# Another build of the node table and the edge records, and two loads per item in the edge loop, in a graph attention and mixture-of-experts kernel

## The chip, the cores and the metric

One core of one Trainium2 chip. The metric is the time of one execution of the program on the device, in microseconds (us), the median of several runs without a recording. Lower is better.

## What is computed

A graph attention layer and then a mixture of experts, each added to its input. The part that the change touches is the first:

```python
x = x + gnn(layernorm(x), edge_attr_16, edge_attr_4, W_n, attn_l, attn_r, attn_m, src, dst)   # 6250 x 256, 200000 edges, dst sorted
x = x + ffn(layernorm(x), router_w, w1, w2, w3)                                             # 8 experts, the best 2

def gnn(feat, e_pro, mask, W_n, attn_l, attn_r, attn_m, src, dst):
    feat_src = (feat @ W_n).reshape(N, 8, 32)
    el = einsum('nhd,hdt->nht', feat_src, attn_l)
    er = einsum('nhd,hdt->nht', feat_src, attn_r)
    em = einsum('ef,hft->eht', e_pro, attn_m)                # e_pro: 16 features of an edge
    e = (einsum(el[src], mask) + einsum(er[dst], mask) + einsum(em, mask)) / 3   # mask: 4 of an edge
    e = where(e > 0, e, 0.2 * e)
    e_exp = exp(e - segment_max(e, dst)[dst])
    a = e_exp / segment_sum(e_exp, dst)[dst]
    return segment_sum(feat_src[src] * a[:, :, None], dst)
```

## The kernel before, in words

Everything is float32. The nodes lie in 49 blocks of 128. Semaphores order the engines; there is no planner, each engine's program is written out by hand. What stands on a queue (SP's and ACT's DMA issues among it) runs in the order of the program, and an instruction that waits holds back all behind it.

*Stage 1, the table build (lines 199 to 490).* SP loads dst, then x (`xall`) in one DMA and its last block in another, W_n and router_w, src, and then edge chunks. ACT issues 24 small DMAs of constants (`bd`, `bm`). PE waits for all 26 of `w_in` (line 442) before it makes the projection weights `wall`. DVE finds which edge begins a node (`pen`), makes 5 of 49 counts, takes `bn_stats` of all 49 blocks (line 398), joins them (`join_stats`), and ACT takes one root over all (line 330). Then block by block: DVE normalizes (`norm`, line 405), PE transposes (`turn`, line 462), ACT copies (`copy_xt`, line 334), PE projects (line 468), DVE copies out (`rows_out`, line 410) to `fo`, of which there are two, and SP stores to `table` in DRAM (line 283). A norm is two blocks ahead of its copy-out. Into the loop are woven 44 more counts on DVE, `count` (line 390): how many dst in a row of 1600 are below a block's end. Every second block there is a chunk of 100 edge columns: SP loads 16 features and 4 mask values per edge, ACT packs (`pack`, lines 348 to 352) src, dst, penalty, an empty word, the mask and the features to records of 24 words, SP stores them to `rec_d`. There are 16 chunks; the program order of SP is two table stores, a chunk store, a chunk load.

*Stage 2 (lines 494 to 635).* PE sums the counts, and a short chain on PE and DVE makes the list of items: 256 successive edges each, 832 of them, which may begin anywhere in the records (`start_i`) and belong to one block (`blk_i`). Then eight w2 matrices are transposed on the way from DRAM to DRAM.

*Stage 3, the edge loop (lines 644 to 1203).* It is unrolled: 52 batches of 16 items. `slot(i, w)` is a batch's turn on each engine. SP's slot (line 796): `records` loads the records of batch +3, item by item (`load_records`, lines 770 and 771: it reads the item's start into a register, checks it, computes an address, issues a DMA of 128 x 192 B), after ACT's `unpack` of the batch before; `penalties` loads `pen_in_rows`; `targets` stores what DVE took out of the records and loads it again, broadcast, as `dst_row`. For `dst_row` waits ACT's `compare` (line 943). POOL gathers table rows for 16 items, two indirect DMAs an item (line 819), at most 36 items ahead of PE's sums. ACT's `unpack` (lines 992 to 998) copies the mask and the features of a batch out of the records, and PE's `turn_e16` (line 826) transposes the features. DVE weighs the gathered rows, PE sums them by one-hot matrices (line 862), DVE adds to the accumulator (line 1163).

*Then* come the router, the sorting of nodes to experts, and the expert tiles. None of it is changed.

## Time and profile before

| | us |
|---|---|
| median of 3 runs (lowest, highest) | 4086.85 (4086.71, 4087.13) |
| the profiled execution's own time | 4127.28 |
| its span | 4125.6 |
| table build, about | 0 to 228 |
| items and w2 | 228 to 291 |
| edge loop | 291 to 2930 |
| router, sorting, experts | 2930 to 4125.6 |

| | PE | weight loads | DVE | ACT | POOL |
|---|---|---|---|---|---|
| busy us in the span | 3054.4 | 2356.6 | 1979.3 | 1623.2 | 1857.8 |
| share | 74% | 57% | 48% | 39% | 45% |

The profile is of one execution of the program. Engines are PE (matmul), PEld (its weight load), DVE, ACT, POOL, and SP, which issues DMAs; a q behind a name (SPq) is the engine's sequencer. "L771" is line 771. In a row of the timeline stand the start, the length, the engine, the line, the operation, the tiles written and read, how many of them were merged (x16), and in brackets how long the engine had been idle and what ended it. "remote" and "issue" stand there where the profile shows no cause. Register steps, semaphore waits and DMA issues are not counted as busy time.

### The profile page before, as it was taken

To read this page: it belongs to the slowest core of one execution; us is meant where nothing else is said; L and a number is where in the kernel's file an instruction comes from. 1 tells how busy PE (TensorE), PEld (TensorE's weight loads), DVE (VectorE), ACT (ScalarE), POOL (GpSimd) and SP (SyncE) were. 2 spreads that over 40 slices of the span, in tenths; PEclk is the share of its full clock that TensorE was granted. 3 is DMA by queue.
4 is the path that set the end of the run, shared out by engine and by line. 5 is a ranking of instruction groups with operands and counts; after the bars stand their busy time and mean duration, and the time that the engine had idled before them with its cause. 6 is when DMAs were issued, how large, how long until landed. Compare 5 with 4: busy or idle time off the path is not lost. (4 is left out here: it accounts for less than half of the span.)

```text
span 4125.6 us, 59259 instructions
## 1 busy us (share of the span) xinstructions
PE 3054.4 (74%) x12566; PEld 2356.6 (57%) x12567; DVE 1979.3 (48%) x5348; ACT 1623.2 (39%) x3631; POOL 1857.8 (45%) x1906
## 2 busy tenths in 40 slices
PE   3541777776777777777677776777765999999997
PEld 1221666565556665665566655555553677777775
DVE  6730555555555555555555555555673122222221
ACT  2311544454455444545544544455432222222221
POOL 0005456666666665666665666666254111111111
PEclk9865677777777777777767778777855999999998
DMA  7834444444444444444444444446564312121123
GB/s 221 258 138 112 123 140 130 131 128 129 131 129 130 131 130 128 132 138 130 130 131 129 130 130 130 130 129 119 75 216 136 91 31 32 31 32 31 31 32 83
DMA packets 309415, 481.35 MB, mean 117 GB/s; under 512 B 161911, under 2 KB 237507, under 8 KB 300366
## 3 DMA queue, kind: packets, MB, share of 16 engines
q0 software_dynamic: 100848, 285.40, 28.1%
q1 hardware_dynamic: 194910, 181.82, 14.5%
q10 hardware_dynamic: 13392, 11.23, 0.9%
q8 instruction: 89, 1.46, 0.2%
q14 instruction: 176, 1.44, 0.1%
HBM read 408.52 MB, written 76.12 MB: 117 GB/s over the span
## 5 line engine op out<-in xcount | busy, mean ns | idle before, releaser
L819 POOL DMA_INDIRECT rows<-table,idx x1664 | 1575.6, 947 | 1063.3 <-issue 445.9
L862 PE MATMUL ps_acc<-rows,hot 128*128 128x264 f32 x3328 | 1260.7, 516 | 538.5 <-DVE acc L1163 496.5
L862 PEld LDWEIGHTS ps_acc<-rows,hot 128*128 128x128 f32 x3328 | 761.9, 253 | 673.1 <-issue 566.6
L1163 DVE TENSOR_TENSOR acc<-acc,ps_acc 128x264 f32 x832 | 355.3, 427 | 987.3 <-remote 659.3
L847 PEld LDWEIGHTS ps_term<-er,hot_t 128*128 128x128 f32 x3328 | 638.1, 247 | 218.5 <-issue 146.5
L847 PE MATMUL ps_term<-er,hot_t 128*128 x3328 | 579.5, 305 | 85.7 <-issue 67.9
L1149 DVE TENSOR_TENSOR rows<-rows,ps_p 128x512 f32<-128x512 f32 x832 | 565.5, 680 | 3.8 <-ACT ps_p L971 0.5
L960 ACT ACTIVATE hot<-iota_row,neg_rel 128x128 f32<-128x128 f32 x1664 | 546.3, 388 | 8.7 <-PE ps_acc L862 8.0
L1730 PE MATMUL ps_h<-w,acc 128*128 x1680 | 528.5, 457 | 0.5 <-ACT acc L1649 0.5
L1642 POOL DMA_INDIRECT x_dram<-acc,to x105 | 161.7, 1540 | 761.8 <-ACT acc L1658 761.8
L935 ACT COPY e_t<-ps_e 128x128 f32<-128x128 f32 x208 | 56.4, 271 | 1021.6 <-remote 978.1
L1730 PEld LDWEIGHTS ps_h<-w,acc 128*128 128x128 f32 x1680 | 302.5, 190 | 158.5 <-issue 36.2
L1743 PE MATMUL ps_y<-w2s,acc 128*128 x1260 | 312.1, 390 | 7.5 <-DMA w2s<-w_t 6.6
L1698 DVE COPY acc<-ps_g 128x256 f32<-128x256 f32 x105 | 44.6, 425 | 521.7 <-PE ps_g L1737 521.7
L1743 PEld LDWEIGHTS ps_y<-w2s,acc 128*128 128x128 f32 x1260 | 231.7, 190 | 85.7 <-issue 43.4
L943 ACT ACTIVATE hot_t<-dst_row,neg_part 128x1024 f32<-128x1024 bf16 x208 | 239.1, 1149 | 34.8 <-DMA dst_row<-rel_d 34.7
L1658 ACT ACTIVATE acc<-ps_y,gate 128x256 f32<-128x256 f32 x105 | 49.8, 475 | 476.2 <-PE ps_y L1743 476.2
L965 ACT ACTIVATE hot<-hot 128x1024 f32<-128x1024 f32 x208 | 219.7, 1056 | 5.0
L949 ACT ACTIVATE hot_t<-hot_t 128x1024 f32<-128x1024 f32 x208 | 217.0, 1043 | 0.2
L839 PE MATMUL ps_term<-bm,e_t 128*128 128x256 f32 x416 | 190.6, 554 | 31.6 <-ACT e_t L935 31.6
L1711 DVE TENSOR_TENSOR acc<-acc,ps_h 128x341 f32<-128x341 f32 x210 | 97.6, 506 | 179.0 <-PE ps_h L1730 179.0
L1666 ACT ACTIVATE acc<-ps_h 128x341 f32<-128x341 f32 x210 | 84.1, 453 | 219.5 <-PE ps_h L1730 219.5
(263 smaller groups left out, 2811.9 us busy)
## 6 DMA issues: line engine op xcount, KB each, us to landing
dst_row<-rel_d SPq DMA_DIRECT2D x52, 1024.0 KB
rows<-table,idx POOLq DMA_INDIRECT x1664
rec<-rec_d SPq DMA_DIRECT2D x832, 24.0 KB
rec_d<-acc SPq DMA_DIRECT2D x16, 1050.0 KB
acc<-slots_x SPq DMA_DIRECT2D x105, 130.0 KB, 2.1
acc<-in_edge_attr_dram SPq DMA_DIRECT2D x16, 700.0 KB
wrow<-in_L_ffn_w_dram ACTq DMA_DIRECT2D x16, 640.0 KB
table<-fo SPq DMA_DIRECT2D x49, 148.0 KB
```

Of the source, the lines that this page charges most:

```text
L819: pool.indirect_dma_start(rows[:, in_ring(k) + j, :], None, table, bass.IndirectOffsetOnAxis(ap=idx[w][:, t:t + 1], axis=0)).then_inc(gath ...
L839: pe.matmul(ps_term[s % 2][:, 0:QT * HT], e16_t[s % 2][:, :], bm[:, :, :].rearrange("p t d -> p (t d)"), start=True, stop=False)
L847: last = pe.matmul(ps_term[s % 2][:, t * HT:(t + 1) * HT], hot_t[s % 2][:, t, :], flat(er[:, ds(b, 1), :]), start=False, stop=(t == QT - 1))
L862: last = pe.matmul(ps_acc[m % 2][:, 0:PW], hot[m // QI % 2][:, m % QI * G + j, :], rows[:, in_ring(i * (2 * NI) + at) + j, 0:PW], start=(j ...
L943: act.activation(hot_t[s % 2][:, :, :], dst_row[s // QUADS][:, s % QUADS * QT:(s % QUADS + 1) * QT, :], ACT.Square, bias=neg_part[:, 0:1]) ...
L949: act.activation(hot_t[s % 2][:, :, :], hot_t[s % 2][:, :, :], ACT.Relu, bias=1.0, scale=-1.0).then_inc(item_made, 1)
L960: act.activation(hot[m // QI % 2][:, t % QT, :], iota_row[:, :], ACT.Square, bias=neg_rel[m // NI][:, t:t + 1]).then_inc(square_ok, 1)
L965: act.activation(hot[s % 2][:, :, :], hot[s % 2][:, :, :], ACT.Relu, bias=1.0, scale=-1.0).then_inc(hot_ok, 1)
L1149: dve.tensor_tensor(r, r, p4, ALU.mult).then_inc(msg_ok, 1)
L1163: dve.tensor_tensor(so_far, so_far, ps_acc[m % 2][:, 0:PW].rearrange("p (h d) -> p h d", h=HEADS), ALU.add).then_inc(added, 1)
L1730: last = pe.matmul(ps_h[2 * m + half][:, 0:HALF], xt[v][:, k * P:(k + 1) * P], flat(w13[:, ds(e, 1), at:at + HALF]), start=(k == 0), stop= ...
L1743: last = pe.matmul(ps_y[:, 0:DIM], ht[v][0:w, c * P:(c + 1) * P], flat(w2s[0:w, ds(e, 1), c * DIM:(c + 1) * DIM]), start=(c == 0), stop=(c ...
```

## The change

- x is loaded in seven groups of seven blocks, each on a semaphore of its own, group 0 as the very first DMA, W_n and router_w right behind it. Statistics, joining, root and reciprocal are made per group: `spread(g)` on DVE after the copy-out of block 7(g-1)+1, `root(g)` on ACT, `roots(g)` on DVE three blocks later.
- The edge features are copied from the input to `e16_d` inside DRAM, in eight DMAs that ACT issues (`copy_e16`), five behind the last five packs and three at the start of stage 2. Records have 8 words; a chunk has 200 columns; there are eight, one every five blocks.
- The counts of odd blocks are made on ACT, as a sum of signs (`Sign` with a threshold lowered by one half, and an accumulator), and repaired in stage 2: s/2 + 800. None is made ahead of the loop.
- `fo` has four buffers; the loops of the build are unrolled.
- In the edge loop SP gets `features(i, w)`: 16 further loads (a register read, a check, an address, a DMA of 128 x 128 B) between `records` and `penalties`, for batch +2. The records' DMAs are 128 x 64 B. ACT unpacks the mask alone. PE's `turn_e16` waits for the features' DMAs.

The diff, cut to its core:

```diff
-CHUNK = 100
+CHUNK = 200
-RC = 4 + T + F
+RC = 4 + T
-EARLY = 5
+FO = 4
+CHUNK_EVERY = 5
+ACT_COUNTS = range(1, BLOCKS, 2)
+E16_PARTS = 8
+E16_EARLY = 5
...
+        def copy_e16(eng, n):
+            lo, hi = n * (EDGES // E16_PARTS), (n + 1) * (EDGES // E16_PARTS)
+            eng.dma_start(e16_d[lo:hi, :].rearrange("r f -> (r f)").rearrange("(a n) -> a n", a=200),
+                          edge16[lo:hi, :].rearrange("r f -> (r f)").rearrange("(a n) -> a n", a=200)).then_inc(e16_out, 16)
...
@@ SP, table build
+                    load_x(0)
+                    sp.dma_start(wall[:, :, 0:DIM], w_n.rearrange("(k p) d -> p k d", p=P)).then_inc(w_in, 16)
+                    sp.dma_start(rt_rows[:, :], router_w).then_inc(w_in, 16)
+                    sp.wait_ge(dst_none, 4)
                     sp.dma_start(dst_sb[0:1, 1:COLS + 1], dst[0:COLS].unsqueeze(0)).then_inc(dst_in, 16)
...
+                    load_x(1)
                     for part_of in SPREAD:
                         sp.dma_start(src_sb[part_of, :], src.rearrange("(p t) -> p t", p=EP)[part_of, :]).then_inc(src_in, 16)
+                    for c in range(2):
+                        load_chunk(c)
+                    for g in range(2, GROUPS):
+                        load_x(g)
+                    for b in range(BLOCKS):
                         sp.wait_ge(f_sb, b + 1)
+                        sp.dma_start(table[b * P:(b + 1) * P, :], fo[:, b % FO, :]).then_inc(f_out[b % FO], 16)
+                        c = chunk_after(b - 1)
+                        if c is not None:
+                            store_chunk(c)
+                            if c + 2 < CHUNKS:
+                                load_chunk(c + 2)
...
@@ ACT, table build
+                    for b in range(BLOCKS):
+                        if b + 2 < BLOCKS:
+                            copy_xt(b + 2)
+                        if b % BC == 2 and b // BC + 1 < GROUPS:
+                            root(b // BC + 1)
+                        c = chunk_after(b)
+                        if c is not None:
+                            pack(c)
+                            if c >= CHUNKS - E16_EARLY:
+                                copy_e16(act, c - (CHUNKS - E16_EARLY))
+                        if b in ACT_COUNTS:
+                            act.wait_ge(signs_ok, ACT_COUNTS.index(b))
+                            count(b)
...
@@ DVE, table build
+                    for b in range(BLOCKS):
+                        if b + 2 < BLOCKS:
+                            norm(b + 2)
+                        if b not in ACT_COUNTS:
+                            dve.wait_ge(cnt_ok, counted)
+                            count(b)
+                            counted += 1
+                        rows_out(b)
+                        g = b // BC + 1
+                        if g < GROUPS:
+                            if b % BC == 1:
+                                spread(g)
+                            if b % BC == 4:
+                                roots(g)
...
@@ ACT, stage 2
+                    for n in range(E16_EARLY, E16_PARTS):
+                        copy_e16(act, n)
...
@@ SP, edge loop
+                    def features(i, w):
+                        after_apart(sp, e16_ps, batches(i, w, QUADS, QUADS))
+                        for u in range(NI):
+                            k0 = sp.value_load(start_i[0:1, ds(batches(i, w, NI, 2 * NI + u), 1)], min_val=0, max_val=EDGES)
+                            sp.dma_start(of_item(e16[w], u).rearrange("p j f -> p (j f)"),
+                                         e16_d[ds(k0, ITEM), :].rearrange("(p j) f -> p (j f)", j=G)).then_inc(e16_in[w], 16)
...
                         if is_batch(i, w, 3):
                             records(i, w)
+                        if is_batch(i, w, 2):
+                            features(i, w)
                         if is_batch(i, w, 1):
                             penalties(i, w)
...
                     load_records(0, 0)
+                    sp.wait_ge(e16_out, 16 * E16_PARTS)
                     all_slots(slot)
...
@@ PE, edge loop
-                        pe.wait_ge(taken_ok, (i + r) * 2 + (s // QUADS + 1))
+                        pe.wait_ge(e16_in[s // QUADS], 16 * NI * (i + r + 1))
...
@@ ACT, edge loop
                         after(act, term_used, batches(i, w, QUADS, QUADS))
-                        after(act, e16_ps, batches(i, w, QUADS, QUADS))
-                        act.copy(mask[w][:, :, :], rec[w][:, :, RC - F - T:RC - F])
-                        act.copy(e16[w][:, :, :], rec[w][:, :, RC - F:RC]).then_inc(taken_ok, 1)
+                        act.copy(mask[w][:, :, :], rec[w][:, :, RC - T:RC]).then_inc(taken_ok, 1)
```

## Rows read from the trace of the kernel before

**Rows 1.** Stretches: length, busy us per engine (instructions), granted clock, DMA share, GB/s.

```profile
112.00:160.00 48.00, 22.94 (x70) 12.62 (x71) 32.56 (x71) 19.79 (x42) 0.00 (x0) 0.81 0.97 309
...
200.00:245.00 45.00, 22.31 (x76) 10.26 (x76) 30.93 (x76) 3.38 (x10) 1.66 (x5) 0.84 0.16 52
```

**Rows 2.** Waits of ACT, 54 to 215 us: in total, times, longest.

```profile
ACT acc L348 <- DMA acc<-in_edge_attr_dram: 59.8, 14, 5.8
```

**Rows 3.** Timeline of the start: start, length, engine, line, operation, idle before.

```profile
9.14 4.75 ACTq L316 DMA_DIRECT2D bm<-in_L_gnn_attn_m_dram  x8
...
32.39 1.09 PE L445 MATMUL ps_w<-ident,wall 128*128 128x128 f32 x4 [32.39 <-DMA rt_rows<-in_L_ffn_router_w_dram]
...
36.43 0.19 ACT L328 COPY rt<-ps_f 128x16 f32<-128x16 f32 x1
...
53.82 0.74 DVE L405 TENSOR_SCALAR xn<-xall,mv,rstd 128x256 f32<-128x256 f32 x2
```

**Rows 4.** Groups by line and shape, 0 to 470 us: count | busy, mean ns.

```profile
L390 DVE TENSOR_SCALAR_CACHE_REDUCE junk<-dst_sb,thr 128x1600 f32<-128x1600 int32 x49 | 91.7, 1872 | 0.1
...
L352 ACT COPY acc<-acc 125x1600 f32<-125x1600 f32 x16 | 24.3, 1518 | 0.0
...
L398 DVE BATCH_NORM_STATS2 stats<-xall x49 | 16.1, 409 | 8.8 <-DMA xall<-in_x_dram 8.8
...
L330 ACT ACT_TABLE_LOAD x1 | 1.3, 1283 | 0.0
```

**Rows 5.** Timeline of DVE in the build: first copy out, both paces, last.

```profile
58.47 0.42 DVE L410 COPY fo<-ps_f 128x256 f32<-128x256 f32 x1 [2.98 <-PE ps_f L468]
...
62.39 0.42 DVE L410 COPY fo<-ps_f 128x256 f32<-128x256 f32 x1 [2.98 <-PE ps_f L468]
...
205.24 0.42 DVE L410 COPY fo<-ps_f 128x256 f32<-128x256 f32 x1
...
208.12 0.42 DVE L410 COPY fo<-ps_f 128x256 f32<-128x256 f32 x1
...
227.14 0.42 DVE L410 COPY fo<-ps_f 128x256 f32<-128x256 f32 x1 [0.92 <-DMA table<-fo]
```

**Rows 6.** DMA issues: count, KB each, us from issue to landing.

```profile
out_dram<-x_dram SPq DMA_DIRECT2D x1, 6250.0 KB, 21.8
```

**Rows 7.** Timeline of SP's queue at the loop's start.

```profile
292.43 41.52 SPq L771 DMA_DIRECT2D rec<-rec_d  x32
...
341.02 0.70 SPq L794 DMA_DIRECT2D dst_row<-rel_d  x1
352.25 61.25 SPq L771 DMA_DIRECT2D rec<-rec_d  x16
...
416.44 0.34 SPq L794 DMA_DIRECT2D dst_row<-rel_d  x1
```

**Rows 8.** Timeline of POOL at the loop's start.

```profile
314.05 1.02 POOL L819 DMA_INDIRECT rows<-table,idx  x1 [26.79 <-DVE idx L1065]
...
392.88 0.95 POOL L819 DMA_INDIRECT rows<-table,idx  x1 [0.30 <-issue]
```

**Rows 9.** Line 771, 292 to 314 us: ns min/median/max, first and last start.

```profile
L771 SPq FUSED_REGOPS  x20: 42/42/47, 292.3 to 313.6; - x20
```

**Rows 10.** The same line, 344 to 403 us.

```profile
L771 SPq MOVE rec<-rec_d x7: 690/700/1387, 350.8 to 400.0; - x7
```

**Rows 11.** Timeline of SP's queue in the steady loop.

```profile
1510.47 36.96 SPq L771 DMA_DIRECT2D rec<-rec_d  x16
...
1562.10 35.72 SPq L771 DMA_DIRECT2D rec<-rec_d  x16
```

**Rows 12.** Groups of POOL, 500 to 2700 us.

```profile
L819 POOL DMA_INDIRECT rows<-table,idx x1413 | 1338.0, 947 | 863.7 <-remote 398.4 <-issue 377.0 <-PE ps_acc L862 88.3
```

**Rows 13.** Timeline of all engines at one pause of the loop.

```profile
1548.58 0.43 DVE L1163 TENSOR_TENSOR acc<-acc,ps_acc 128x264 f32 x1 [4.12 <-remote]
...
1549.18 0.95 POOL L819 DMA_INDIRECT rows<-table,idx  x1 [2.76 <-remote]
```

More of the change, by code:

```diff
@@ L226, in gnn_moe_kernel, with chunk_after @@
             f_ps, f_sb = sem("f_ps"), sem("f_sb")
-            f_out = [sem("f_out0"), sem("f_out1")]
+            f_out = [sem(f"f_out{u}") for u in range(FO)]
+            def chunk_after(b):
+                c, left = divmod(b, CHUNK_EVERY)
+                return c if left == 0 and c < CHUNKS else None
             with nc.Block() as block:
@@ L297, in _ @@
-                    with sp.Fori(2 * CHUNKS, BLOCKS - 1, 2) as b:
-                        for u in range(2):
-                            store_rows(b + u, u)
-                    sp.wait_ge(f_sb, BLOCKS)
-                    sp.dma_start(table[(BLOCKS - 1) * P:ROWS, :], fo[:, 0, :]).then_inc(f_out[0], 16)
-                    sp.wait_ge(f_out[0], 16 * (BLOCKS // 2 + 1))
-                    sp.wait_ge(f_out[1], 16 * (BLOCKS // 2))
+                    for c in range(2):
+                        load_chunk(c)
@@ L304, in _ @@
+                    for u in range(FO):
+                        sp.wait_ge(f_out[u], 16 * len(range(u, BLOCKS, FO)))
                     for u in range(2):
                         sp.wait_ge(rec_out[u], 32 * (CHUNKS // 2))
-                    sp.wait_ge(pads, 16)
+                    sp.wait_ge(pads, 32)
                 @block.scalar
@@ L317, in _, with root @@
                                      attn_m.rearrange("h f t -> f h t")).then_inc(w_in, 16)
-                    act.wait_ge(pad_ok, 2)
-                    act.dma_start(rec_d[EDGES:EDGES + PAD, :].rearrange("(a n) c -> a n c", a=64), pad_rec[:, :, :]).then_inc(pads, 16)
+                    def root(g):
+                        act.wait_ge(var_ok, g + 1)
+                        act.activation(rstd[:, g * BC:(g + 1) * BC], mv[:, g * BC:(g + 1) * BC, 1], ACT.Sqrt, bias=eps[:, 0:1]).then_inc(std_ok, 1)
+                    root(0)
                     act.wait_ge(wt_ps, 1)
@@ new lines, in count @@
+                    def count(b):
+                        act.activation(junk_a, dst_sb[:, 1:COLS + 1], ACT.Sign, bias=thr_a[:, b:b + 1], scale=-1.0,
+                                       accum_out=cnt[:, b + 1:b + 2]).then_inc(signs_ok, 1)
+                    act.wait_ge(pad_ok, 2)
+                    act.dma_start(rec_d[EDGES:EDGES + PAD, :].rearrange("(a n) c -> a n c", a=64), pad_rec[:, :, 0:RC]).then_inc(pads, 16)
+                    act.dma_start(e16_d[EDGES:EDGES + PAD, :].rearrange("(a n) c -> a n c", a=64), pad_rec[:, :, RC:RC + F]).then_inc(pads, 16)
@@ L386, in _ @@
                     dve.tensor_scalar(pen[:, :], pen[:, :], BIG, -BIG, ALU.mult, ALU.add).then_inc(pen_ok, 1)
-                    def count(b):
-                        dve.tensor_scalar(junk[:, :], dst_sb[:, 1:COLS + 1], thr[:, ds(b, 1)], 0.0, ALU.is_lt, ALU.add,
-                                          accum_out=cnt[:, ds(b + 1, 1)]).then_inc(cnt_ok, 1)
-                    for b in range(EARLY):
-                        count(BLOCKS - EARLY + b)
-                        dve.wait_ge(cnt_ok, b + 1)
@@ L416, in _ @@
-                    norm(0, 0)
-                    norm(1, 1)
-                    for u in range(2):
-                        dve.wait_ge(xt_ps, u + 1)
-                        norm(2 + u, u)
-                        rows_out(u, u)
-                    with dve.Fori(2, BLOCKS - 3, 2) as b:
-                        for u in range(2):
-                            dve.wait_ge(xt_ps, b + (u + 1))
-                            norm(b + (2 + u), u)
-                            dve.wait_ge(cnt_ok, b + (u + EARLY - 2))
-                            count(b + (u - 2))
-                            dve.wait_ge(f_out[u], b * 8)
-                            rows_out(b + u, u)
@@ L564, in _ @@
                 def _(dve):
+                    signs = cnt[:, 1 + ACT_COUNTS.start:1 + BLOCKS:2]
+                    dve.wait_ge(signs_ok, len(ACT_COUNTS))
+                    dve.tensor_scalar(signs, signs, 0.5, COLS / 2.0, ALU.mult, ALU.add).then_inc(cnt_ok, 1)
                     dve.wait_ge(b_const, 2)
@@ L713, in one_ahead @@
                 return (i, 0) if w else (i - 1, 1)
+            e16_in = [sem(f"e16_in{w}") for w in range(2)]
             (prep_ok, stored, prep_ps, rows_ok, idx_ok, taken_ok, rel_ok, first_ok, far_ok, item_made, e16_ps, e16_sb, term_ps, term_used, scored, xs_ps,
```

209 lines of the change are left out of this document (94 added, 115 removed).

## The prediction

> **What bounds the kernel now.** I read the stretches first, then the waits inside the table build, then the queue of SP in the loop. The profiled execution took 4127.28 us around a span of 4125.6; the median of the runs without a recording is 4086.85, 40.4 us less. The sum below is made against the profiled one as a difference, and the difference is put on the median.
>
> The table build ends at about 228 us. In its middle the DMA engines are 97% busy at 309 GB/s, while PE, DVE and ACT are not [rows 1]; ACT waits 59.8 us for edge chunks before it can pack [rows 2]. So from 60 to about 189 us transfers set the pace: the loads of 12.8 MB of edge features, and 19.2 MB of records that carry them again. The last blocks, without chunks, run at a pace of their own: one block in 2.88 us [rows 5], a norm, a count and a copy-out on DVE in turn, or 3.92 us [rows 5] while the granted clock is low and DVE waits for PE. Before that comes a start of 53.8 us, in which PE waits until 32.39 for router_w, queued behind the whole of x, and DVE cannot normalize before all 49 blocks have their statistics [rows 3].
>
> In the loop, POOL's gathers take 947 ns each, 1413 of them in 2200 us, hence 32 a batch and one batch in 2200/1413 x 32 = 49.8 us [rows 12]. Every four items or so POOL and DVE pause for 3 to 4 us, until something that the trace doesn't name arrives [rows 13]. SP issues the 16 record loads of a batch within 37 us, and starts the next 16 after 51.6 us [rows 11]: one load in 2.3 us. Where POOL gathers nothing, a load costs SP 21.3/19 = 1.12 us [rows 9]. During a long run of gathers, 314 to 393 us [rows 8], each of SP's small steps takes 0.70 us or twice that, even a MOVE between registers [rows 10], and a load takes 49.2/6 = 8.2 us.
>
> **The change, part by part.**
>
> Start. x comes in seven loads, w and router_w right behind the first. The constants' DMAs on ACT are all issued by 9.14 + 4.75 = 13.9 us [rows 3]; they should land by 16 to 17. From PE's first transpose to the finished weights it was 36.43 + 0.19 - 32.39 = 4.2 us, so the weights are there at about 21. From the first norm to the first copy-out it was 58.47 - 53.82 = 4.65 us [rows 3, 5]; two pads' DMAs and the penalties on DVE come in between, about 1.5. First copy-out at 27 against 58.5, 31 us earlier; bounds 26 (a chunk load delays a small DMA) to 34.
>
> Pace. Now 227.14 - 58.47 = 168.7 us for 48 steps [rows 5], 3.51 each. The features no longer pass through SBUF: the DMA work falls from some 42 MB to 30, of which 4.8 are moved out of the stage, and the chunks (8, of 200 columns) have 160 us. I take transfers off the path. What is late next is the cycle norm, turn, project, copy-out. It was 2.88 with a count and hardly shorter without, as PE is in it: 48 x 2.77 = 133. To this come the statistics, which stood ahead of the blocks and are now among them: seven at 16.1/49 = 0.33 [rows 4] and the joining, 3.6 us a group, of which the next block's PE work hides some 1 us: 6 x 2.6 = 16. Reciprocals 3. On ACT a count costs between the 1.52 us of its copy of the same 1600 elements and DVE's 1.87 [rows 4]; I take 1.65 (the nearest kind is the copy, plus an accumulator read). A count with a copy of xt is 2.0 of some 5.6 us for two blocks, so it is hidden, except where a pack (three copies of 200 elements and one of 800, some 1.8 us at the rate of the 1600-element copy and 0.15 of fixed cost each, an estimate) or a root with up to two table loads of 1.28 [rows 4] meets it: 8 us in all. If five blocks run at the slow cadence: 5 x 1.15 = 6. Sum 166 us. Bounds 155 to 182, the upper with the low clock for a third of the blocks. So the last copy-out is at 27 + 166 = 193 against 227.1: -34 us for the whole build, start and pace together, bounds -46 to -18. The queues passed: SP issues loads x2 to x6 before the first store, four fo buffers cover that; ACT issues five of the eight copies of features, each an instruction of under 1 us, behind packs.
>
> The stage after it. Three of eight copies, 4.7 MB, run beside the counting and the first weight loads. The nearest row is a copy inside DRAM, 6250 KB in 21.8 us [rows 6]: 16 us, most of it before the first w2 rows are asked for. +0 to +10, I take +3; DVE's repair of the signs is 0.3 in it.
>
> The Trainium skill, page "DMA: Bandwidth & Descriptors", section on why a DMA increments its semaphore by 16, says that a copy uses the largest number of engines up to 16 that divides its slowest dimension. Here that is 200, thus 10 engines, while the copy in [rows 6] has 800. By that rule the three copies take 16/10 of the time, 26 us instead of 16, and the sum would move by about +5. No row here shows ten engines at work.
>
> The loop's start. SP issues records 0 and 1, then targets 0, records 2, penalties 0, targets 1; the dst_row of batch 0 leaves at 341.02 and that of batch 1 at 416.44, with 61 us for the 16 loads between [rows 7]. The change puts the features of batch 0 ahead of targets 0 and those of batch 1 ahead of penalties 0. Behind each stand the penalties and targets, and for those wait ACT (compare), then PE and DVE. At the quiet price each is 16 x 1.12 = 18 us. At the price within the gathers the first takes 60, but then the second run of records falls after 393 us, where loads are quick again, and 30 is left in all. Bounds 5 (gathers, 40 us a batch, are what the start waits for anyway) to 36; I take +23.
>
> The steady loop. ACT loses a copy of 0.6 us a batch and is half idle: 0. The records shrink to 8 words and features come straight: more but smaller packets, DMA is half busy: 0 to +1 us a batch. What counts is SP: 32 loads a batch instead of 16. At the quiet price 32 x 1.12 = 36 us and about 7 for penalties and targets, 43 of 49.8: it fits, barely. So 0 for my forecast, and this is where I choose. Its bounds are the rivals.
>
> Why I choose the quiet price: a step that touches no memory should not depend on gathers, so what stretches a MOVE to 0.70 us is likely the recording of each step. The one place where SP's long steps stand on the path is 352 to 402 us, seven loads in 49 + 8 us instead of 8. That is about 49 us too much, and without a recording the kernel is 40.4 us shorter.
>
> Sum: -34 + 3 + 23 + 0 = -8, rounded to 4080. With the bounds of the parts: 4050 to 4120 in this case.
>
> **The rivals.**
>
> 1. *SP becomes the bound of the loop* (slower). Condition: long steps are real. Price: gathers run 32 x 1.25 = 40 us of a batch. In the 37 us of 16 loads about 29.7 are such time and 7.3 quiet, which carries 6.5 loads; the other 9.5 take 3.1 us each. With 32 loads: 40/3.1 = 12.9 within gathers, 19.1 x 1.12 = 21.4 quiet, and 7.6 for the rest: 69 us a batch, +19.2, times 50 = +960; with build and start 4087 - 34 + 3 + 30 + 960 = 5046. If the sixteen more all fall in quiet time, 16 x 1.12 = 18 less 6 of slack, +12 a batch: 4690; if each costs 2.3 us, +31 a batch: 5640. For it: [rows 10, 11], and that the pauses [rows 13] must be real, as without them the kernel would be much shorter than 4087. Against: the argument above.
> 2. *The start hides the features* (faster): the gathers of batch 0 fill 40 us anyway, so +5 instead of +23, and the build gives 42: 4087 - 42 + 0 + 5 = 4050.
> 3. *Long steps are half real*: semaphores and DMA issues slow down, register steps don't. A load within the gathers 1.8 us: 40/1.8 = 22, the other 10 cost 11, 51 + 4 of waits = 55 us, less what overlaps, +3 a batch: about 4230.
> 4. *The copies or the packing still hold the build*: then no gain there, and the start's price stands: 4087 + 23 + 3 = 4113. It lies in the range.
>
> **How the numbers follow.** Forecast 0.35 (of it 0.13 faster, 0.14 the same, 0.08 slower), rival 1 0.32, rival 2 0.18 (all faster), rival 3 0.10, rival 4 0.05. Faster by over 0.2% (8 us, about what can be told from no change): 0.31; within: 0.14; slower: 0.55. The range goes from 4040 to the centre of rival 1, 5050: half of rival 1 and a tenth of rival 2 are left out, together under 0.2. The forecast's own range is 4050 to 4120.
>
> **What would show it.** The first copy-out (line 410's successor) near 27 us and the last near 193; DMA share under 0.7 in between. SP's 32 loads of a batch within some 40 us in a recording would confirm the forecast; a batch of 65 to 70 us with PE, DVE and ACT waiting for dst_row, and a loop of some 3500 us, is rival 1. If the recorded execution is then far longer than the unrecorded ones, SP's long steps came from the recording. The prediction is wrong if the gap between the blocks stays above 3.3 us with a high clock, or if the gathers themselves slow down.

## The result, and the profile after

The changed kernel takes 4695.82 us (median; 4691.28 to 4716.02), the kernel before 4086.78 beside it: 1.149 times as long, 95% interval 1.145 to 1.153, or 609 us more. In the profiled executions (spans 4125.6 and 4697.9) POOL's timeline splits the difference into three parts: the first gather starts at 295.46 instead of 314.05, 18.6 us earlier; from there to the end of the last gather it takes 3206.3 us instead of 2612.0, 594.3 more; what follows takes 1196.1 instead of 1199.5. In this execution the build brought 18.6 us of the 31 that were forecast for it and the stage behind it; the loop lost thirty times as much.

The stretches of the build after, in the columns of [rows 1]:

```profile
112.00:160.00 48.00, 30.76 (x72) 16.27 (x72) 26.36 (x81) 18.26 (x34) 0.00 (x0) 0.61 0.51 170
200.00:245.00 45.00, 17.82 (x64) 9.36 (x62) 10.01 (x24) 7.07 (x15) 3.00 (x7) 0.59 0.70 231
```

The DMA share fell from 0.97 to 0.51: transfers no longer hold the blocks. The rows of the timeline that answer to [rows 3, 5], first PE's first transpose of the weights, then DVE's first and last copy-out of a block, then the first gather [rows 8]:

```profile
25.07 1.08 PE L472 MATMUL ps_w<-ident,wall 128*128 128x128 f32 x4 [25.07 <-DMA bm<-in_L_gnn_attn_m_dram]
33.62 0.43 DVE L435 COPY fo<-ps_f 128x256 f32<-128x256 f32 x1 [1.33 <-PE ps_f L500]
202.66 0.42 DVE L435 COPY fo<-ps_f 128x256 f32<-128x256 f32 x1
295.46 1.02 POOL L855 DMA_INDIRECT rows<-table,idx  x1 [26.26 <-DVE idx L1099]
```

In the loop, SP's queue over one batch (the timeline of SP, to be held against [rows 11]):

```profile
2000.43 0.34 SPq L827 DMA_DIRECT2D dst_row<-rel_d  x1
2001.70 26.49 SPq L796 DMA_DIRECT2D rec<-rec_d  x16
2029.57 28.46 SPq L804 DMA_DIRECT2D e<-e_d  x16
2058.15 0.57 SPq L816 DMA_DIRECT2D pen_in_rows<-pen_d  x1
2059.05 0.34 SPq L824 DMA_DIRECT2D rel_d<-rel_b  x1
2059.44 0.41 SPq L825 DMA_DIRECT2D pen_d<-pen_s  x1
2061.00 0.34 SPq L827 DMA_DIRECT2D dst_row<-rel_d  x1
2062.28 26.51 SPq L796 DMA_DIRECT2D rec<-rec_d  x16
```

One block follows the other without a gap; 55 of 60.6 us go into the 32 loads, 1.72 us each. POOL meanwhile stands still, for PE (timeline and groups of POOL, 600 to 3300 us):

```profile
2051.02 0.94 POOL L855 DMA_INDIRECT rows<-table,idx  x1 [0.31 <-issue]
2065.18 0.94 POOL L855 DMA_INDIRECT rows<-table,idx  x1 [13.22 <-PE ps_acc L898]
```

```profile
L855 POOL DMA_INDIRECT rows<-table,idx x1409 | 1331.6, 945 | 1368.7 <-PE ps_acc L898 833.9 <-issue 366.2 <-remote 168.6
```

PE waits for ACT, and ACT for what SP brings late (waits, 600 to 3300 us: in total, times, longest):

```profile
PE ps_acc L898 <- ACT hot L1001: 681.8, 44, 18.2
ACT pen_t L1025 <- DMA pen_in_rows<-pen_d: 675.3, 44, 17.4
...
ACT hot_t L979 <- DMA dst_row<-rel_d: 7.9, 19, 0.9
```

In each of 44 batches ACT stands 15.3 us before `pen_in_rows`, which SP issues behind the 32 loads; for `dst_row`, which follows it, it hardly waits any more.

A gather still takes 945 ns [rows 12], but a batch now 2700/1409 x 32 = 61.3 us instead of 49.8. The view that says most is one that the prediction makes no use of: what SP itself waits for. Before, 600 to 2700 us (in total, times, longest):

```profile
SPq L98 <- ACT e L998: 139.0, 34, 7.5
SPq L98 <- DVE pen_s L1061: 65.5, 19, 4.5
SPq L98 <- DMA pen_d<-pen_s: 12.3, 11, 1.6
```

and after, 600 to 3300 us:

```profile
SPq L102 <- DMA pen_d<-pen_s: 48.4, 44, 1.5
```

Before, SP waited 216.8 us in 2100/49.8 = 42 batches: 5.1 us of slack a batch (0.3 of it for its own transfer). The change put 16 loads into it. After, SP waits for no engine any more, only for its own transfer.

### The profile page after: what moved, and what is told of

Its sections match the earlier page's. It is cut to its first block and busy times, and to the rows that moved or that the text cites. A ratio compares the mean times of both kernels' runs of the same rounds, so it can differ in the third digit from the quotient of the medians.

```text
span 4697.9 us, 63277 instructions
## 1 busy us (share of the span) xinstructions
PE 3094.1 (66%) x12566; PEld 2390.9 (51%) x12567; DVE 1940.0 (41%) x5344; ACT 1620.6 (34%) x3584; POOL 1852.6 (39%) x1907
## 2 busy tenths in 40 slices
DMA packets 425412, 468.99 MB, mean 100 GB/s; under 512 B 281607, under 2 KB 355203, under 8 KB 418062
## 5 line engine op out<-in xcount | busy, mean ns | idle before, releaser
L898 PE MATMUL ps_acc<-rows,hot 128*128 128x264 f32 x3328 | 1301.9, 530 | 1020.5 <-ACT hot L1001 763.5
L898 PEld LDWEIGHTS ps_acc<-rows,hot 128*128 128x128 f32 x3328 | 776.7, 258 | 1165.8 <-issue 1055.8
L883 PEld LDWEIGHTS ps_term<-er,hot_t 128*128 128x128 f32 x3328 | 659.8, 255 | 182.3 <-issue 103.1
L883 PE MATMUL ps_term<-er,hot_t 128*128 x3328 | 595.1, 311 | 55.7 <-issue 36.9
L1025 ACT COPY pen_t<-pen_in_rows 128x256 f32<-128x256 f32 x52 | 23.8, 459 | 769.1 <-DMA pen_in_rows<-pen_d 769.1
L1692 ACT ACTIVATE acc<-ps_y,gate 128x256 f32<-128x256 f32 x105 | 49.8, 475 | 473.4 <-PE ps_y L1777 473.4
L1007 ACT ACTIVATE ps_p<-weight 128x256 f32<-128x256 f32 x52 | 20.2, 388 | 507.0 <-DVE rows L1183 346.2
L875 PE MATMUL ps_term<-bm,e_t 128*128 128x256 f32 x416 | 167.5, 493 | 28.7 <-ACT e_t L971 28.6
```

The source lines that it names most:

```text
L875: pe.matmul(ps_term[s % 2][:, 0:QT * HT], e16_t[s % 2][:, :], bm[:, :, :].rearrange("p t d -> p (t d)"), start=True, stop=False)
L883: last = pe.matmul(ps_term[s % 2][:, t * HT:(t + 1) * HT], hot_t[s % 2][:, t, :], flat(er[:, ds(b, 1), :]), start=False, stop=(t == QT - 1))
L898: last = pe.matmul(ps_acc[m % 2][:, 0:PW], hot[m // QI % 2][:, m % QI * G + j, :], rows[:, in_ring(i * (2 * NI) + at) + j, 0:PW], start=(j ...
```

## The experiments

The median of the kernel before lay between 4082 and 4123 us in the experiments, which ran on three chips and in several visits (a visit is one session on a chip), so each kernel is compared with the runs of before that ran beside it.

**1. Only two batches of features loaded** (changed kernel).

```
                         if is_batch(i, w, 3):
                             records(i, w)
-                        if is_batch(i, w, 2):
+                        if i < 0:
                             features(i, w)
...
-                        pe.wait_ge(e16_in[s // QUADS], 16 * NI * (i + r + 1))
+                        pe.wait_ge(e16_in[s // QUADS], 16 * NI)
```

> The changed kernel, but the features are loaded for the first two batches only; PE turns those again in every batch, so the scores are not the reference's. SP has 16 loads a batch again. Theory S (SP's queue is the bound of the changed loop: 32 loads of 1.7 us and 4.8 us of rest make its 60.2 us a batch): the batch falls back to 49.8 us, the build stays 18.6 us earlier than before (first gather 295.5 against 314.05), so 4087 - 19 = 4068 (4055 to 4085). Rival O (the new place of the waits, such as PE's for a semaphore of the features, holds the loop): unchanged, 4696. Rival D (smaller records, more small packets): about half of the loss stays, some 4400.

Measured 4133.93 against 4123.01: ratio 1.002 (0.9999 to 1.004). Rivals O and D are out: without the loads the 600 us are gone, and in the profiled execution a batch takes 49.6 us (mean of the distances between every 32nd gather, from the sixth batch on). The expected 19 us of gain did not come. The first gather is at 300.5, but the first four batches take 61.2 + 73.3 + 64.8 + 51.0 = 250.3 us where before took 40.1 + 66.3 + 65.3 + 49.1 = 220.8: the two batches of features that this kernel still loads stand in the loop's start and cost 29.5 us there. So the run measures, beside the loop, the term "loop's start" of the prediction.

**2 to 4. The loads, their reads and their transfers, each alone, in the kernel before.**

```
+                    def extra(i, w):
+                        after_apart(sp, e16_ps, batches(i, w, QUADS, QUADS))
+                        for u in range(NI):
...
+                            k0 = sp.value_load(start_i[0:1, ds(k, 1)], min_val=0, max_val=EDGES)
+                            sp.dma_start(spare[:, u % 8, :],
+                                         rec_d[ds(k0, ITEM), :].rearrange("(p j) c -> p (j c)", j=G)[:, 0:G * F]).then_inc(spare_in[u // 4 % 2], 16)
```

The second of the three kernels has only the read, the third only the transfer, at a fixed address.

> The kernel before, plus 16 loads a batch into a spare tile that nobody reads, each with its own register read, of 128 x 128 bytes like the loads of the features, at the place in SP's order where the change puts them. Nothing else is touched. Theory S: this alone makes the whole loss: 32 x 1.73 + 4.8 = 60.2 us a batch, 10.4 to 10.9 more in some 50 batches, 4087 + 545 = 4630 (4600 to 4680). Rival O: nobody waits for the new loads, so 4087 to 4110.

> The kernel before, plus only the 16 register reads of those extra loads (read, register operation and range assertion: three of a load's six steps), without any transfer. Theory S by the number of steps: a read costs about half of a load's 1.73 us, so SP needs 16 x 1.73 + 16 x 0.87 + 4.8 = 46.4 us of the 49.8 us batch, it still fits: 4085 to 4110. If SP had no slack at all before, +14 us a batch: 4780. Rival D (the transfers cost the time, not the steps): 4087.

> The kernel before, plus the 16 extra transfers a batch of 128 x 128 bytes into the spare tile, at fixed addresses, so each costs SP one issuing step instead of six. Theory S: 16 x 0.4 to 0.7 = 6 to 11 us more for SP, 16 x 1.73 + 11 + 4.8 = 43.5 of 49.8 us, it fits: 4085 to 4110. Rival D (more small packets on the DMA engines slow the gathers or the records): as slow as with the full loads, about 4630.

Measured, beside 4123.01: 4741.51 (ratio 1.152, 1.148 to 1.156), 4316.07 (1.044, 1.038 to 1.051) and 4154.48 (1.009, 1.006 to 1.012). The first alone makes the whole loss, although no other engine waits for its data: it is the work on SP's queue. Rival D, the number of packets, is out: the same transfers without the reads cost 31 us. All three cost more than expected: the loads 618 us against at most 593, the transfers 31 against at most 23, and the reads 193 against at most 23, which is the one that was wrong in kind. It had left SP 49.8 - 16 x 1.73 - 4.8 = 17 us of slack, from the average price of a load in the changed loop; SP had 5.1. The waits of SP in that kernel, 600 to 2700 us, show that the reads used it up:

```profile
SPq L98 <- DMA pen_d<-pen_s: 34.0, 24, 2.2
```

**5. Where the loads stand in SP's order** (changed kernel; features behind penalties and targets instead of ahead of them).

```
-                        if is_batch(i, w, 2):
-                            features(i, w)
                         if is_batch(i, w, 1):
                             penalties(i, w)
                         if is_batch(i, w, 2):
                             targets(i, w)
+                        if is_batch(i, w, 2):
+                            features(i, w)
```

> The changed kernel with the loads of the features moved behind the penalties and targets in SP's order; their number stays. Theory S (throughput of SP): SP's work a batch is the same, 60 us, so the time is that of the changed kernel, 600 above the kernel before (570 to 640). Rival O (it is the targets that come late because the features stand ahead of them): most of the loss goes, 0 to 100 above the kernel before.

Measured 4727.57 against 4081.78, 1.158 (1.152 to 1.164). This other order brings nothing back; SP's work a batch is the same.

**6. Fewer steps a load.**

```
-                            k0 = sp.value_load(start_i[0:1, ds(batch * NI + u, 1)], min_val=0, max_val=EDGES)
+                            k0 = sp.value_load(start_i[0:1, ds(batch * NI + u, 1)])
```

and the same for the features.

> The changed kernel with the register reads of SP (records and features) without their range assertion: a load has five steps instead of six. In a quiet stretch the step is 0.07 us of the load's 1.10; in a run of gathers each step costs as much as any other. Theory S, which counts steps: about 0.2 us less of 1.73 a load, 32 x 0.2 = 6.4 us a batch, 50 batches: 320 less, thus 290 above the kernel before (200 to 400). Rival (only the transfers count): 600 above, unchanged.

Measured 4172.47 against 4081.78, 1.022 (1.016 to 1.028): 91 us above, better than expected. The trace shows that two steps of each load went, not one: the assertion and the register operation ahead of it. The direction is theory S's; the size was estimated too small, by a factor of two in the steps.

**7. ACT issues the features** (changed kernel; the 16 loads in one block behind ACT's unpacking).

```
+                                if v == QUADS - 1 and u == 2 and is_batch(i, w, 2):
+                                    for q in range(QUADS):
+                                        features(i, w, q)
```

> The changed kernel with the 16 feature loads of a batch issued from ACT's queue, in one block behind the unpacking, instead of SP's. SP is back to 16 loads. Theory S, if the gathers lengthen ACT's steps too: 16 x 1.7 = 28 us more on ACT beside some 27 us of its own work a batch, 55 us, and the block delays the one-hot tiles that PE waits for: 250 to 500 above the kernel before. If ACT's steps keep the quiet price, 18 us more, 45 of 49.8 us fit: 0 to 60 above.

Measured 4688.80 against 4081.78, 1.148 (1.145 to 1.152), 607 above, beyond the upper end. The timeline of ACT shows the block (13 of its 16 loads) and, in brackets, how long ACT computed nothing:

```profile
1499.87 14.76 ACTq L1023 DMA_DIRECT2D e<-e_d  x13
1514.68 0.69 ACT L985 ACTIVATE hot<-iota_row,neg_rel 128x128 f32<-128x128 f32 x2 [20.15 <-issue]
```

and ACT's waits, 600 to 2700 us, show that it does so in each of 34 batches, 671.5/34 = 19.8 us:

```profile
ACT hot L985 <- issue: 671.5, 34, 20.7
```

Here SP has slack again (it waits 417 us for DVE and ACT in that stretch) and the time is lost where ACT computes nothing. That this block is what holds the loop is argued from these waits, not tested: another queue doesn't help when the engine behind it has work that others wait for. That the loads in small portions would do better wasn't tried.

**8 to 10. The price by itself.** Three small kernels compute nothing of the reference; they only run SP's loads and POOL's gathers. SP has the same code in all of them; m_loads has no gathers, and m_burst differs from m_both in POOL's wait:

```
                     k0 = sp.value_load(start[0:1, ds(k, 1)], min_val=0, max_val=EDGES - 256)
                     sp.dma_start(rec[:, k % 16, :], edge16[ds(k0, 256), :].rearrange("(p j) c -> p (j c)", j=2)).then_inc(rec_in[g], 16)
...
-                    if k % 8 == 0 and k >= 32:
-                        pool.wait_ge(got[g], k // 32 * 128)
+                    if k % 8 == 0 and k >= 8:
+                        pool.wait_ge(got[(g + 3) % 4], (k - 8) // 32 * 128 + 128)
```

> A kernel of its own, which computes nothing of the reference (it copies x into the output): SP issues 1024 loads of 128 x 128 bytes, each with a register read, as in the loop, with waits only for a ring of 16 tiles; no other engine works. It measures the quiet price. Every theory expects 1024 x 1.10 to 1.12 = 1127 to 1147 us plus some 30 to 45 us of start: 1160 to 1190.

> The same, and beside it POOL issues 1024 gathers of 128 rows (of 1 KB here) one after the other, 1.25 us each, so for some 1280 us; the two share nothing, no semaphore and no tile. Theory S (gathers lengthen each step of SP, and PE need not take part): at 2.0 to 2.8 us a load SP gets through 460 to 640 of them in that time and does the others at 1.12 us: 1740 to 1940 us in all; at the 8.2 us of the long run of gathers at the loop's start 2280. Rival Q (long steps come from something else in the loop, PE's or ACT's traffic, or from the recording): the longer of the two streams, 1310 to 1330 us.

> The small kernel with both streams, but POOL waits after every eight gathers until they have landed, as its pauses in the loop. 128 bursts of 8 x 1.40 us and a pause of some 2.5 us: gathers end near 1750 us. Rule A (one step of SP for every gather, as in the run without pauses, 1.12 us a load in the pauses): 3.6 loads a burst, 460 in that time, 560 more at 1.12 us: 2360 to 2420 us. Rule B (the first gathers behind a pause leave SP's steps short, as the loop's 2.3 us a load suggests): 750 loads in that time, 2050 to 2100 us.

Measured 1168.14 us (loads alone), 2385.61 (both), 1535.13 (both, gathers in bursts of eight). Loads alone are as expected. With gathers in an unbroken run the kernel takes twice as long, 2385.17 us with a recording and 2386.05 without, so the recording is not the cause, and no other engine works here; rival Q is out. It is more than the 1740 to 1940 us expected from the loop's prices, and nearest to the 2280 from the 8.2 us of the loop's start. The steps of a load with the gathers beside it, by line (ns min/median/max; read, then transfer):

```profile
L69 SPq TENSOR_LOAD <-start x143: 700/700/700, 104.6 to 1297.5; - x143
L69 SPq FUSED_REGOPS  x143: 699/700/724, 106.0 to 1298.9; - x143
L69 SPq SEQ_ASSERT  x142: 699/700/728, 107.4 to 1291.9; - x142
...
L70 SPq MOVE rec<-in_edge_attr_dram x143: 700/700/703, 101.8 to 1294.7; - x143
L70 SPq DMA_DIRECT2D rec<-in_edge_attr_dram x143: 699/700/728, 103.2 to 1296.1; - x143
```

and without gathers:

```profile
L61 SPq SEQ_ASSERT  x894: 18/18/18, 100.0 to 1099.1; - x179
L61 SPq TENSOR_LOAD <-start x894: 262/269/278, 100.6 to 1099.7; - x179
...
L62 SPq MOVE rec<-in_edge_attr_dram x894: 29/29/37, 100.2 to 1099.2; - x179
L62 SPq DMA_DIRECT2D rec<-in_edge_attr_dram x894: 337/338/347, 100.2 to 1099.3; - x179
```

A move between registers takes 700 ns instead of 29. 143 loads in 1200 us are 8.4 us a load, six steps of 1.40; and 1.40 us is the distance of the gathers too:

```profile
599.14 1.09 POOL L56 DMA_INDIRECT rows<-in_x_dram,idx  x1 [0.30 <-issue]
600.54 1.09 POOL L56 DMA_INDIRECT rows<-in_x_dram,idx  x1 [0.30 <-issue]
601.94 1.09 POOL L56 DMA_INDIRECT rows<-in_x_dram,idx  x1 [0.30 <-issue]
```

SP gets one step for each gather, and the gathers themselves are longer than the 0.94 us that they take in bursts. With a wait for all eight gathers between bursts, a load takes (1200 - 100)/925 = 1.19 us, nearly the quiet price (by line, 100 to 1200 us):

```profile
L70 SPq DMA_DIRECT2D rec<-in_edge_attr_dram x925: 1/337/705, 100.2 to 1199.3; - x185
```

Theory B was nearer than A (2050 to 2100 expected), and still far too high. The loads are all issued by 1242 us; what ends at 1535 is the gathers with their pauses. The expectations of the next runs reckon with 1.35 us a load, which the trace doesn't show; with 1.19 their sums leave SP still more room.

**11 to 14. Is it POOL's queue running ahead, and do bursts help in the loop?** The kernels called paced, and m_ahead in its own way, make POOL wait for the gathers of two items that stand three and four back; a_burst waits before every fourth item for all that went before:

```
                             after_apart(pool, acc_done, k - ROW_ITEMS + 1)
+                            if k % 2 == 0 and k >= 4:
+                                pool.wait_ge(gathered[(k - 4) // 2 % (4 * QUADS)], (k - 4) // (2 * NI) * 64 + 64)
```

```
+                            if k % QI == 0 and k >= QI:
+                                pool.wait_ge(gathered[(k // QI - 1) % (2 * QUADS)], (k - QI) // (2 * NI) * 128 + 128)
```

> The small kernel with both streams; POOL waits before every fourth gather until the gathers have landed that stand five to eight places back, so its queue cannot run further ahead, but need not pause. Theory Q2 (POOL's queue running ahead holds the other queues up): loads at 1.2 to 1.4 us, gathers at 1.25: 1300 to 1500 us. Theory G (a gather under way holds them up, only a pause helps): as without waits, 2385 us.

> The changed kernel, with its 32 loads a batch, and the same wait of POOL in the loop: before every second item until the gathers of the items three and four back have landed (a semaphore for every two items, so DVE waits for two). Theory Q2: a load costs SP 1.35 us, 32 x 1.35 + 4.8 = 48 us, within the 49.8 us: the loss goes, 20 below to 60 above the kernel before. Theory G: 600 above, unchanged.

> The kernel before with that wait alone. Theory Q2: SP has more slack; the loop's start gets quicker, as the seven loads of 8.2 us there become short (up to 45 us less), and if PE's small steps are held up too, the pauses of POOL behind every eight gathers shrink (2.5 us each, up to 100 us less in all). 30 to 150 below the kernel before. Theory G: within 5 of it, or up to 100 above if the waits cost POOL time.

> The changed kernel; POOL waits before every fourth item until all gathers of the four items before have landed, so it runs in bursts of eight with about 2.9 us between. Theory L (a burst that starts with nothing under way leaves SP's steps short, as in the small kernel): SP needs 32 x 1.35 + 4.8 = 48 us, POOL 32 x 1.25 + 4 x 2.9 = 51.6 us and sets the pace: 1.8 us a batch more than before, 90 less the 19 of the build: 40 to 130 above the kernel before. Theory W (in the loop other work takes part in it): a load stays at 1.7 us and the time about 600 above.

Measured: m_ahead 2389.81; a_paced 4728.21 against 4087.98 (1.159, 1.153 to 1.165); b_paced 4079.94 (0.9985, 0.997 to 1.0004); a_burst 4773.74 against 4120.03 (1.158, 1.153 to 1.162). Theory Q2 falls: limiting how far POOL's queue runs ahead changes nothing in the small kernel and nothing in the changed one. Theory L falls too: a_burst makes POOL stop and wait for all its gathers before every burst of eight, and a batch takes 63.4 us, no less than without. So what spares SP in the small kernel does not carry over to the loop. Counted over the first 1.25 us of each gather, SP starts 5.7 to 6.3 steps in each of the eight gathers of a burst in m_burst, but in a_burst 6.5 and 5.7 in the first two behind a pause, 3.4 and 2.2 in the next two and 1.1 to 1.7 in the others.

**15 to 17. Versions that keep one load per item.** The first takes only the statistics by group and the counts on ACT from the change:

```
-CHUNK = 200
+CHUNK = 100
-RC = 4 + T
+RC = 4 + T + F
-CHUNK_EVERY = 5
+CHUNK_EVERY = 3
...
+                        act.copy(to[:, :, 4 + T:RC], e16_st[u][0:EP, :].rearrange("p (t f) -> p t f", f=F)).then_inc(rec_ok, 1)
```

The second puts records and features into two planes of one tensor, so that one transfer fetches both:

```
-    rec_d = dram("rec_d", (EDGES + PAD, RC))
-    e16_d = dram("e16_d", (EDGES + PAD, F))
+    both_d = dram("both_d", (2, EDGES + PAD, F))
+    rec_d, e16_d = both_d[0], both_d[1]
...
+                            sp.dma_start(rec[w][:, u, :, :],
+                                         both_d[:, ds(k0, ITEM), :].rearrange("a (p j) c -> p a (j c)", j=G)).then_inc(rec_in[w], 16)
```

> The kernel before with two parts of the change: x in seven groups with own statistics, and half of the counts on ACT (four fo buffers too). The features are packed into records of 24 words as before, 16 chunks of 100 columns, one after every third block, and the loop has one load per item. Theory S: the loop is that of before. The build gains its earlier start (25 us as in the changed kernel), but the transfers (42 MB, 309 GB/s at most: 136 us) and 24 us more of packing on ACT take a part: 5 to 22 us below the kernel before, 15 taken. Rival O (what was changed around the loop's start makes the loss): over 100 us above the kernel before.

> The changed kernel with one load per item again, but without packing of features: records and features lie in two planes of one DRAM tensor, rows of 16 words in both (half of a record row is unused), features are copied in DRAM as in the change, and one transfer of 128 x 2 x 128 bytes fetches both. ACT copies the features out of the tile as before. Theory S: the loop costs 49.8 us a batch again, its start too (40, 66, 65, 49), and the build's 18.6 us stay: 19 below the kernel before on the same chip (28 below to 5 above, if the issuing step is longer for twice as many packets). Rival D (number of small packets): about 400 to 600 above.

> The kernel with the two planes (20 below the kernel before) with that wait. Theory Q2: what the wait brings comes on top: 50 to 170 below the kernel before. Theory G: 20 below.

Measured: build_only 4107.38 against 4122.33, ratio 0.995 (0.994 to 0.997); planes 4102.38 against the same, 0.994 (0.992 to 0.996), 20 us below; planes_paced 4066.23 against 4087.98, 0.995 (0.992 to 0.997), 22 below, so the wait adds nothing that can be told. The first two are as theory S had it, the third as theory G. planes moves nearly as many small packets as the changed kernel (268311 under 512 bytes against 281607, before 161911, from the pages), and SP has its slack back (its waits, 600 to 2700 us):

```profile
SPq L102 <- ACT e L1025: 157.7, 34, 7.5
SPq L102 <- DVE pen_s L1088: 56.1, 18, 4.4
SPq L102 <- DMA pen_d<-pen_s: 16.0, 12, 1.5
```

planes is 0.6% faster than the kernel before, and faster than the changed kernel.

## Why the prediction was wrong, step by step

**The step that failed** is the term of the steady loop, taken as 0 because 32 loads at the quiet price, 36 us, and 7 for the rest fit into 49.8 us. It measured 61.3 - 49.8 = 11.5 us a batch: SP's 32 loads took 55 us, not 36, and with the rest they do not fit. What chose that price is the passage "why I choose the quiet price". It had two arguments. The first: a step that touches no memory should not depend on gathers. The small kernel shows a register move at 700 ns beside gathers and 29 without. The second: the profiled execution was 40.4 us longer than the median, and the recording's long steps would make about 49 us. But this gap is most likely one between chips or visits: beside the experiments the kernel before had medians of 4082 to 4123 us and single unrecorded executions up to 4131. And recording did not lengthen the other kernels so: in the fourteen others of this loop the recorded execution lay between 41 us below and 20 us above the median of the unrecorded ones (4699.82 within 4691 to 4716 for the changed kernel). A difference of 1% between executions on unknown chips was no evidence, and the agreement of 40 with 49 an accident. With that argument gone, [rows 10, 11] and the pauses pointed to rival 1, which is what happened; its chance of 0.32 and the range that reached to it were worth more than the forecast.

**Rival 1** named the mechanism, the place and the sign: SP's queue the bound, PE, DVE and ACT waiting behind it (for `pen_in_rows`, though, and not for the dst_row that it named). Its price was too high, 69 us a batch against 61.3, 5046 against 4696. The term that was mis-sized is "the other 9.5 take 3.1 us each" for loads within gathers. In the changed kernel's batch of 61.3 us, 40 are gathers, about 5 go into penalties and targets, and the 16.3 us left carry 16.3/1.10 = 14.8 loads; the other 17.2 take 40/17.2 = 2.3 us. Counted over the first 1.25 us of each gather (600 to 3300 us), SP starts some 6 steps in each of the first two behind a pause, 4.1 and 2.7 in the next two, and 1.5 to 1.8 from the fifth on, so its price in a batch hangs on how the gathers are grouped.

The bound that held was the lower one, "all sixteen more fall in quiet time, 18 less 6 of slack, 4690". A reason can be given, though no run tests it alone: the gathers of a batch are always 32, whatever SP has to do. Once SP is the bound, each further microsecond of the batch is one in which POOL waits, so added work is done at the quiet price. With SP's 5.1 us of slack (49.8 - 5.1 = 44.7 us of need) this gives for the batches with more work on SP:

```
                       added to SP's queue, quiet price      worked out   measured, us a batch
b_extra_fixed          16 x 0.38 =  6.1                      50.8         50.4
b_extra_reads          16 x 0.57 =  9.1                      53.8         53.3
b_extra_loads          16 x 1.10 = 17.6                      62.3         61.7
changed kernel         16 x 1.10 = 17.6                      62.3         61.4
a_no_assert            17.6 - 32 x 0.28 = 8.6                53.3         51.2
```

The quiet prices of the read and the transfer, 0.57 and 0.38 us, are the distances of these steps within a load in the kernel without gathers; 0.28 is 1.10 less the 0.82 of a load without assertion. In b_extra_fixed's own trace the transfers most often stand 0.47 us apart, which would make its batch 52.2. The rule was found after the runs and fits five of them within 2.1 us; it was not put to a test of its own.

**The start.** First copy-out at 33.62, not 27, and outside the bounds of 26 to 34 us of gain: 58.47 - 33.62 = 24.9. The term that was mis-sized is the landing of the constants: the sum had them there by 16 to 17 us, but PE's first transpose waits for the bm constants until 25.07. ACT had issued them by 13.7, as counted; the DMA engines were full by then, with x and the first chunks (14 to 20 us, in the columns of [rows 1]):

```profile
14.00:20.00 6.00, 0.00 (x0) 0.00 (x0) 3.75 (x6) 1.31 (x2) 0.00 (x0) 1.00 1.03 237
```

From there it went as counted: 8.6 us to the copy-out against 4.2 + 4.65.

**The pace.** 202.66 - 33.62 = 169.0 us for 48 steps, 166 forecast, within 155 to 182. Transfers did leave the path. But the granted clock was 0.61 in the middle stretch, where 0.81 stood before, which the forecast had counted for five blocks only. What that costs can be read from the other runs, as seven kernels have the very same build (granted clock from 60 to 185 us; us from the first to the last copy-out; first gather):

| | clock | 48 steps | first gather |
|---|---|---|---|
| a_act_features | 0.86 | 156.6 | 280.2 |
| a_no_assert | 0.85 | 159.9 | 280.2 |
| a_paced | 0.77 | 165.4 | 289.7 |
| changed kernel | 0.73 | 169.0 | 295.5 |
| a_burst | 0.66 | 173.4 | 299.4 |
| a_few_features | 0.66 | 175.9 | 300.5 |
| a_features_last | 0.65 | 173.5 | 297.2 |

The first, fourth and sixth of them in the columns of [rows 1]:

```profile
60.00:185.00 125.00, 70.39 (x232) 38.56 (x232) 82.55 (x250) 57.03 (x106) 0.00 (x0) 0.86 0.48 161
60.00:185.00 125.00, 72.59 (x198) 38.84 (x198) 76.98 (x236) 50.70 (x96) 0.00 (x0) 0.73 0.48 160
60.00:185.00 125.00, 75.05 (x187) 39.97 (x186) 73.98 (x226) 49.38 (x93) 0.00 (x0) 0.66 0.49 161
```

The DMA share is nearly the same in all three, and the pace goes with the clock: the 48 steps take 12 us less at 0.86 than at the 0.73 of the changed kernel's profile. Without its 6 us for the slow cadence the forecast is 160, already more than the 156.6 at 0.86, so that 166 lies near 169.0 is partly luck. In this execution the last copy-out came 24.5 us earlier instead of 34; in the two with the highest clock the first gather came 34 us earlier than in the kernel before, about what was forecast.

**The stage after it.** From the last copy-out to the first gather 86.9 us before and 92.8 after: +5.9 where +3 was taken, within 0 to 10. The three late copies landed 8.0, 12.2 and 16.1 us after their issue (by line, issue at 205.5 to 206.7):

```profile
L206 ACTq DMA_DIRECT2D e_d<-in_edge_attr_dram x3: 524/610/1407, 205.5 to 206.7; - x3
...
DMA to landing us min/median/max: 8.0/12.2/16.1
```

```profile
q10 hardware_dynamic: 144, 4.80, 24.2%
```

The second view is the DMA queues, 200 to 260 us: packets and MB of ACT's queue. The three copies landed within 17.3 us of the first issue for 4.7 MB, and the sum's 16 came from a copy inside DRAM at the full rate. The Trainium skill, "DMA: Bandwidth & Descriptors", section on why a DMA increments its semaphore by 16, would have had it at 26 us with ten engines. The rule there goes by the pattern as the instruction carries it, and the prediction took the 200 that the program writes. The trace does not agree with that reading: these copies ran about as fast as one on all engines. Their 144 packets are 96 of 50000 bytes and 48 of 4 bytes, so each copy went out in 32 large pieces with 16 small ones, and not as 200 rows of 8000 bytes.

**The loop's start.** +23 taken, bounds 5 to 36; measured by itself 29.5 (experiment 1), where only this part of the loop's added loads was left. It more than cancels the build's 18.6, and a kernel with this start and a loop at the old pace is within 0.4% of before, near the forecast's -8 us; but the loop did not keep its pace.

**Rival 2** is out by that 29.5. **Rival 3**, half-real steps, is out: register steps are as long as the others. **Rival 4** is out by build_only and planes: the build's part is worth 15 to 22 us when the loop keeps one load per item.

## What to carry to other kernels

Ask the profile what the *queue* waits for before adding to it: its waits for other engines, per batch, are all the slack there is, and beyond it every step cost about its quiet price here. Count an issue with a run-time address as all its sequencer steps, and try to fetch two things with one descriptor shape (here two planes of one tensor) before issuing twice. Do not explain a 1% difference between two executions by the recording unless both come from the same chip and visit. When transfers leave the path of a stage, ask what comes next on it: here the pace went with PE's granted clock, and 48 steps of the same build took from 156.6 to 175.9 us.

## What the runs showed of the hardware

Beside an unbroken run of gathers on POOL, every step of SP's sequencer takes 0.70 us plus 0.70 until the next, one step for each gather, whether it reads memory, moves a register or issues a transfer: 8.4 us a load instead of 1.10. The gathers pay too, 1.09 us instead of 0.94. With POOL waiting for its gathers after every eight, a load takes 1.19 us in the small kernel. In the loop the same wait does not help, and a limit on how far POOL's queue runs ahead helps in neither. What the two streams share, and what in the loop, PE's and ACT's queues among it, makes SP's steps long again after two or three gathers, stays open.
